# A new step order for a Mamba-2 decoder layer in fp32: output product ahead, decays one step later

## The chip, the cores and the metric

The kernel runs on one core of one Trainium2 chip. The metric is the time of one execution on the device, in microseconds. The engines are TensorE (PE; its weight loads are PEld), VectorE (DVE), ScalarE (ACT), GpSimd (POOL) and SyncE (SP), which here issues all transfers. Each engine runs its own instructions in the order written; they meet by semaphores.

## The reference

One decoder layer on x of 2 x 256 tokens by 512 features. It has a state-space attention (128 heads of 64, 8 groups of 16 heads), a quantised product with a context, and a block-diagonal GELU network behind a permutation. Nearly all the time is the first:

```
h = rmsnorm(x) * norm_w;  gate, hBC, dt = h @ in_proj_w.T
hBC = silu(causal_conv(hBC, 4 taps));  hid, B, C = hBC
dt = softplus(dt + dt_bias);  A = -exp(A_log)
M = (C B^T) * exp(segsum(A dt))          # per head, chunks of 128
y = M (hid dt) + C state exp(cumsum)  + D * hid
y = groupnorm(y * silu(gate)) * gnorm_w  # over the 1024 channels of a group
out = x + y @ out_proj_w.T
```

## The kernel before, in words

Channels lie on partitions, 512 tokens on the free axis. Each of the 8 groups has 8 tiles of 128 channels (CT = 8), so 64 steps of two heads each. The first and the last group are written out, groups 1 to 6 are one loop over n, with a body of the eight steps t. fp32 products are made of two fp32r parts: ScalarE rounds a weight tile (`cast`, L591; `cast_out`, L599), GpSimd subtracts to get the rest (`split`, L452; `split_out`, L462), and TensorE makes three products per pair (`split3`, L1147 to L1149). A projection is twelve matmuls of 128x512, an output product (`out_tile`) as many.

Step (n, t) holds stages of several tiles, each with a lag: `lagged(n, t, 2)` is the tile two steps back. For a tile the stages are: the projections of its hidden part h and its gate g; ScalarE's first tap (`tap0`, L611), VectorE's other three (L873), tanh (L618) and `conv_silu` (L882); TensorE's transpose (`turn`, L1217) and VectorE's `turned` (L900); the decay rows, loaded to `e` (L364), masked by GpSimd (`mask_rows`, L472), exponentiated by ScalarE (`exps`, L639), and multiplied by the scores, one third by GpSimd (`decays_off`, L483) and two thirds by VectorE (`decays_diagonal`, L926); the two heads' products (`outputs`, L1256 and L1259) into ps_y; `skip_and_gate` (L953 and L956); ScalarE's `z_high_and_square` (L646, L652), VectorE's `z_low` (L962), GpSimd's `add_square` (L490); and the output product into four banks that gather a group. At a group's end `token_sums` (L1268), `mean_square` (L967), `group_rms` (a pow, L494) and four `add_output` (L971) bring it to the residual. B and C of the next group are two more projections, in steps 3 and 5 (B_STEP, C_STEP). `masked_scores` (L911, L914) and `group_params` (L938, L939) belong to t = 0, the end of the group to t = 2.

The order of a step on each engine is written by hand in its `step` function. On TensorE: project h(t), turn(t-1), outputs(t-2), out_tile(t-3), project g(t), and B or C. On GpSimd: the splits of the next step's tiles, decays_off(t-1), split_out(t-2), mask_rows(t), add_square(t-2). On ScalarE: the tanh of g(t-1), casts of the next step's tiles, tap0(t), exps(t-1), tanh(t), z_high_and_square(t-2), cast_out(t-2). On VectorE: gated(t-1) (L892), taps(t), turned(t-1), skip_and_gate(t-2), conv_silu(t), z_low(t-2), decays_diagonal(t-1). Two PSUM banks (ps_in) take the projections in turn, so a projection waits until what used its bank two tiles ago is read (`bank_taken_from`). Rings: six weight tiles, four output weight tiles, four sets of rows.

In the first group GpSimd also rounds the quantised context (`context`, L502 to L506), one tile per step. Behind the last group it makes eight one-hot matrices (L567, L569) ahead of `group_rms`.

## Time and profile before

| | |
|---|---|
| median of 3 runs | 943.29 us (942.54 to 943.3) |
| the profiled execution | 941.07 us, span 939.3 us |
| TensorE busy | 821.1 us, 87% |
| VectorE busy | 696.5 us, 74% |
| GpSimd busy | 624.8 us, 67% |
| ScalarE busy | 542.9 us, 58% |
| mean granted clock of TensorE | 0.933 |

The span goes from the first to the last instruction. Busy shares are means over stretches with different limits, so they only say where to look. A row of a timeline gives the start and the length of an instruction (or of several of a kind that follow each other, with their count), and in brackets the idle time before it and what released it. A granted clock of 1.00 is 2.4 GHz, 0.50 is 1.2 GHz.

### The profile page before, as it was taken

How to read it: one execution, taken by the hardware profiler on the slowest of the kernel's cores; microseconds unless marked ns; L12 is line 12 of the kernel's file. 1: busy time of each engine (PE TensorE's matmuls, PEld its weight loads, DVE VectorE, ACT ScalarE, POOL GpSimd, SP SyncE). 2: the span in 40 equal slices, each digit the busy share in tenths (PEclk: the TensorE clock that was granted, in tenths of full speed). 3: DMA queues.
4: the chain of work that ended last, by engine and by line, in shares of the span. 5: the costliest groups of instructions: out<-in, count | busy, mean ns of one | idle time of the engine just before them, and what ended most of it. 6: DMA issues, size and time to landing. Idle time of an engine off the chain costs nothing.

```text
span 939.3 us, 14298 instructions
## 1 busy us (share of the span) xinstructions
PE 821.1 (87%) x4158; PEld 639.1 (68%) x4158; DVE 696.5 (74%) x912; ACT 542.9 (58%) x1124; POOL 624.8 (67%) x522
## 2 busy tenths in 40 slices
PE   4769898899989998999899998999899989994368
PEld 3547766677767776777677776777687767773155
DVE  6767578588958896797868895879589777672653
ACT  2357566465647664676656574666476665762253
POOL 3578999666856776576756785687667675767220
PEclk9889999899989998999989998999899999998579
DMA  5245344233434353433433343435243343300001
GB/s 189 90 152 201 115 145 146 90 135 123 150 100 147 108 169 107 145 131 126 145 109 133 112 148 134 134 106 172 79 145 134 127 142 124 116 31 22 1 0 45
DMA packets 44048, 111.11 MB, mean 118 GB/s; under 512 B 5748, under 2 KB 6644, under 8 KB 44020
## 3 DMA queue, kind: packets, MB, share of 16 engines
q1 hardware_dynamic: 44020, 110.76, 35.3%
q8 instruction: 14, 0.23, 0.1%
q14 instruction: 14, 0.11, 0.0%
HBM read 109.30 MB, written 1.44 MB: 118 GB/s over the span
## 4 chain that ended last, share of the span: by engine, by line
PE 45%; DVE 27%; issue 13%; ACT 7%; POOL 6%; DVEq 1%; DMA 0%; ACTq 0%; SPq 0%; POOLq 0%
PE ps_in L1147 9%; PE ps_in L1148 8%; PE ps_in L1149 8%; DVE hid L873 6%; PE ps_o L1147 4%; PE ps_o L1148 3%; PE ps_o L1149 3%; DVE z L956 3%; PE ps_y L1256 3%; DVE e L926 3%; DVE hdt L900 2%; DVE z L953 2%; ACT hid L611 2%; DVE bc L882 2%; PE ps_t L1217 1%
## 5 line engine op out<-in xcount | busy, mean ns | idle before, releaser
L1147 PE MATMUL ps_in<-h_hi,w_hi 128*128 128x512 f32 x560 | 232.2, 415 | 22.4 <-DVE gate L892 11.9
L1148 PE MATMUL ps_in<-h_lo,w_hi 128*128 128x512 f32 x560 | 228.4, 408 | 0.0
L1149 PE MATMUL ps_in<-h_hi,w_lo 128*128 128x512 f32 x560 | 227.8, 407 | 0.0
L462 POOL TENSOR_TENSOR wo_lo<-rawo,wo_hi 128x512 fp32r<-128x512 f32 x64 | 112.8, 1763 | 151.1 <-ACT wo_hi L599 97.5
L873 DVE SCALAR_TENSOR_TENSOR hid<-ps_in,curc,hid 128x510 f32<-128x510 f32 x186 | 138.9, 747 | 93.6 <-ACT hid L611 88.5
L452 POOL TENSOR_TENSOR w_lo<-raw,w_hi 128x512 fp32r<-128x512 f32 x144 | 188.9, 1332 | 15.7 <-ACT w_hi L591 15.6
L639 ACT ACTIVATE e<-e,nag 128x256 f32<-128x256 f32 (+1 forms) x512 | 183.6, 443 | 12.0 <-POOL e L472 12.0
L1147 PEld LDWEIGHTS ps_in<-h_hi,w_hi 128*128 128x128 f32 x560 | 111.2, 199 | 50.4 <-issue 24.2
L611 ACT ACTIVATE hid<-ps_in,curc 128x512 f32<-128x512 f32 x62 | 48.1, 776 | 150.4 <-PE ps_in L1149 139.4
L1149 PEld LDWEIGHTS ps_in<-h_hi,w_lo 128*128 128x128 f32 x560 | 111.4, 199 | 24.7
L1148 PEld LDWEIGHTS ps_in<-h_lo,w_hi 128*128 128x128 f32 x560 | 111.7, 199 | 22.9
L483 POOL TENSOR_TENSOR e<-e,gm 128x512 f32<-128x512 f32 x64 | 89.9, 1405 | 54.8 <-ACT e L639 54.7
L1147 PE MATMUL ps_o<-wo_hi,z_hi 128*128 128x512 f32 x256 | 107.7, 421 | 0.6 <-DVE gate L892 0.6
L646 ACT ACTIVATE z_hi<-z,curs 128x512 fp32r<-128x512 f32 x64 | 46.4, 725 | 103.4 <-DVE z L956 103.4
L1148 PE MATMUL ps_o<-wo_lo,z_hi 128*128 128x512 f32 x256 | 100.6, 393 | 0.0
L1149 PE MATMUL ps_o<-wo_hi,z_lo 128*128 128x512 f32 x256 | 100.5, 393 | 0.0
L926 DVE TENSOR_TENSOR e<-e,gm 128x1024 f32<-128x1024 f32 x64 | 93.2, 1457 | 4.4 <-ACT e L639 4.4
L472 POOL TENSOR_SCALAR_AFFINE_SELECT e<-e 128x512 f32<-128x512 f32 x128 | 91.7, 739 | 0.0
L1256 PE MATMUL ps_y<-e,hdt 128*64 128x256 f32 x512 | 81.2, 396 | 6.7 <-POOL e L483 6.4
L591 ACT ACTIVATE w_hi<-raw 128x512 fp32r<-128x512 f32 x144 | 84.3, 621 | 0.0
L490 POOL TENSOR_TENSOR sqsum<-sqsum,sq 128x512 f32<-128x512 f32 x56 | 71.8, 1283 | 6.6 <-ACT sq L652 6.6
L962 DVE SCALAR_TENSOR_TENSOR z_lo<-z,curs,z_hi 128x512 fp32r<-128x512 f32 x64 | 56.9, 889 | 12.9 <-ACT z_hi L646 12.9
(209 smaller groups left out, 1275.2 us busy)
## 6 DMA issues: line engine op xcount, KB each, us to landing
e<-acs_rows SPq DMA_DIRECT2D x64, 768.0 KB, 4.4
raw<-in_w_in SPq DMA_DIRECT2D x144, 256.0 KB, 4.7
rawo<-in_w_out SPq DMA_DIRECT2D x64, 256.0 KB, 2.6
craw<-in_ctx SPq DMA_DIRECT2D x8, 256.0 KB, 3.1
res<-in_x SPq DMA_DIRECT2D x4, 256.0 KB, 3.1
out_x<-res SPq DMA_DIRECT2D x4, 256.0 KB, 2.2
acs_rows<-z SPq DMA_DIRECT2D x3, 128.0 KB, 1.9
rawo<-in_w_dt SPq DMA_DIRECT2D x1, 256.0 KB, 4.3
```

What stands on the lines that cost most here:

```text
L452: pool.tensor_tensor(w_lo[:, slot, :], raw[:, slot, :], w_hi[:, slot, :].bitcast(F32), ALU.subtract).then_inc(s_lo, 1)
L462: pool.tensor_tensor(wo_lo[:, q % WO_RING, :], rawo[:, q % RAWO_RING, :], wo_hi[:, q % WO_RING, :].bitcast(F32), ALU.subtract).then_inc(s_ ...
L472: last = pool.affine_select(out=d, in_=d, compare_op=ALU.is_ge, fill=MASKED, base=0, pattern=[[0, 2], [0, BATCH], [1, P]], channel_multipl ...
L483: pool.tensor_tensor(o, o, gm[:, 1, :, :].rearrange("p b i -> p (b i)").unsqueeze(1) .broadcast_to([P, 2, BATCH * P]), ALU.mult).then_inc( ...
L591: act.activation(w_hi[:, slot, :], raw[:, slot, :], ACT.Copy).then_inc(s_hi, 1)
L639: last = act.activation(a, a, ACT.Exp, bias=nag[:, 2 * b + late, h:h + 1])
L873: last = dve.scalar_tensor_tensor(y[:, :, a:], src[:, :, 0:SEQ - a], par[:, at + 3 - a:at + 4 - a], y[:, :, a:], ALU.mult, ALU.add)
L926: dve.tensor_tensor(a, a, g, ALU.mult).then_inc(s_ma, 1)
L1147: pe.matmul(dst, lh, rh, start=first, stop=False)
L1148: pe.matmul(dst, lh, rl, start=False, stop=False)
L1149: return pe.matmul(dst, ll, rh, start=False, stop=last)
L1256: last = pe.matmul(ps_y[rows_, at:at + SEQ], w, e[:, q % E_RING, hh, 0:2, b, :], start=True, stop=False, skip_group_check=True)
```

## The change

The stages stay the same; their order and their lags change. The gate's projection moves a step back: step t projects h(t), then B or C (now at t = 4 and 6), then g(t-1). On TensorE the output product of t-3 goes ahead of turn(t-1) and outputs(t-2), the scores move to t = 1, and token_sums stands behind the outputs of t = 2. decays_off and decays_diagonal get a lag of 2, at the start of the step, gated as well; add_square a lag of 3. On ScalarE the second and third cast go behind z_high_and_square, cast_out ahead of tap0. On VectorE conv_silu(t) stands before skip_and_gate, masked_scores and group_params move to t = 1, mean_square to the end of t = 2, and the four add_output to t = 3, ahead of the taps. The context's three instructions per tile move from GpSimd in the first group to VectorE in the last, with the conversion of the permutation; the one-hot matrices move to VectorE, behind mean_square. The last square is no more added by GpSimd: the last token sums take both parts. The first group has four steps of lead instead of three, `LEAD` is one tile instead of two. SP loads input weights two steps ahead as before. `following(n, t)` is the list of step t+1's tiles; `extra_of(n, t)` names B or C.

```diff
-LEAD = 2
+LEAD = 1
...
-B_STEP, C_STEP = 3, 5
+B_STEP, C_STEP = 4, 6
...
 def step_tiles(n, t):
...
+    extra = extra_of(n, t)
+    back = (0, ("C0", 0)) if is_first(n) and t == 0 else (n, ("g", t - 1)) if t else (n - 1, ("g", CT - 1))
+    return [(n, ("h", t))] + ([(n, extra)] if extra else []) + [back]
...
             def step(n, t):
-                if t == 2 and not is_first(n):
+                tiles = following(n, t)
+                lead = is_first(n) and t < 4
+                if t == 3 and not is_first(n):
                     group_rms(n - 1)
-                ahead = (n, t + 1) if t + 1 < CT else (n + 1, 0)
-                tiles = [] if is_last(n) and t + 1 == CT else step_tiles(*ahead)
-                lead = is_first(n) and t < 3
-                if tiles:
-                    split_in(ahead[0], tiles[0])
-                m, q = lagged(n, t, 2)
-                if tiles:
-                    split_in(ahead[0], tiles[1])
...
+                if not lead:
+                    decays_off(*lagged(n, t, 2))
...
-                if not (is_first(n) and t < 2):
-                    decays_off(*lagged(n, t, 1))
-                    rows_arrived(n, t)
-                    split_out(m, q)
-                    mask_rows(n, t)
-                if len(tiles) > 2:
-                    split_in(ahead[0], tiles[2])
+                split_in(*tiles[0])
+                m, q = lagged(n, t, 3)
                 if q and not lead:
                     add_square(m, q)
...
+                if not (is_first(n) and t < 2):
+                    rows_arrived(n, t)
...
+                if len(tiles) > 1:
+                    split_in(*tiles[1])
...
+                if not (is_first(n) and t < 2):
+                    mask_rows(n, t)
+                if not lead:
+                    split_out(*lagged(n, t, 2))
+                if len(tiles) > 2:
+                    split_in(*tiles[2])
...
             def step(n, t):
-                ahead = (n, t + 1) if t + 1 < CT else (n + 1, 0)
-                tiles = [] if is_last(n) and t + 1 == CT else step_tiles(*ahead)
-                extra = {B_STEP + 1: ("B", B_STEP), C_STEP + 1: ("C", C_STEP)}.get(t)
-                extra = None if is_last(n) else extra
-                lead = is_first(n) and t < 3
-                m, q = lagged(n, t, 2)
-                if not (is_first(n) and t == 0):
-                    gate_tanh(*lagged(n, t, 1))
-                if tiles:
-                    cast_in(ahead[0], tiles[0])
-                if extra:
-                    tap0(n, extra)
-                if tiles:
-                    cast_in(ahead[0], tiles[1])
+                tiles = following(n, t)
+                extra, earlier = extra_of(n, t), extra_of(n, t - 1)
+                lead = is_first(n) and t < 4
+                if not (is_first(n) and t < 2):
+                    gate_tanh(*lagged(n, t, 2))
+                cast_in(*tiles[0])
+                if earlier:
+                    conv_tanh(n, earlier)
+                if not lead:
+                    cast_out(*lagged(n, t, 2))
                 tap0(n, ("h", t))
-                if extra:
-                    conv_tanh(n, extra)
...
                 if not lead:
                     exps(*lagged(n, t, 1))
                 conv_tanh(n, ("h", t))
...
+                if extra:
+                    tap0(n, extra)
                 if not lead:
-                    z_high_and_square(m, q)
+                    z_high_and_square(*lagged(n, t, 2))
+                for tile in tiles[1:]:
+                    cast_in(*tile)
...
             def step(n, t):
-                extra = {B_STEP + 1: ("B", B_STEP), C_STEP + 1: ("C", C_STEP)}.get(t)
-                extra = None if is_last(n) else extra
-                lead = is_first(n) and t < 3
-                m, q = lagged(n, t, 2)
-                if t == 0:
+                extra, earlier = extra_of(n, t), extra_of(n, t - 1)
+                lead = is_first(n) and t < 4
+                if t == 0 and not is_first(n):
                     conv_params(n)
                 if t == 2:
-                    if not is_first(n):
-                        mean_square(n - 1)
                     ssd_params(n)
-                if not (is_first(n) and t == 0):
-                    gated(*lagged(n, t, 1))
-                if extra:
-                    taps(n, extra)
+                if not (is_first(n) and t < 2):
+                    gated(*lagged(n, t, 2))
+                if t == 1 and not is_first(n):
+                    group_params(n)
+                if not lead:
+                    decays_diagonal(*lagged(n, t, 2))
+                if earlier:
+                    conv_silu(n, earlier)
+                if t == 3 and not is_first(n):
+                    dve.wait_ge(s_r, n)
+                    dve.wait_ge(s_ou, CT * n)
+                    for k in range(TT):
+                        add_output(k)
...
                 taps(n, ("h", t))
-                if extra:
-                    conv_silu(n, extra)
...
                 if not lead:
                     turned(*lagged(n, t, 1))
-                    skip_and_gate(m, q)
-                conv_silu(n, ("h", t))
...
+                conv_silu(n, ("h", t))
+                if not lead:
+                    skip_and_gate(*lagged(n, t, 2))
...
                 if not lead:
-                    z_low(m, q)
-                    decays_diagonal(*lagged(n, t, 1))
-                if t == 0 and not is_first(n):
-                    group_params(n)
+                    z_low(*lagged(n, t, 2))
+                if extra:
+                    taps(n, extra)
+                if t == 1 and not is_first(n) or t == 2 and is_first(n):
                     masked_scores(n)
                 if t == 2 and not is_first(n):
-                    dve.wait_ge(s_r, n)
-                    dve.wait_ge(s_ou, CT * n)
-                    for k in range(TT):
-                        if is_first(n - 1):
-                            dve.wait_ge(s_res, TT)
-                        add_output(k)
...
+                    mean_square(n - 1)
+                if is_last(n):
+                    context(t)
...
             last_m = GROUPS - 1
+            gated(last_m, CT - 2)
+            decays_diagonal(last_m, CT - 2)
+            turned(last_m, CT - 1)
             skip_and_gate(last_m, CT - 2)
-            gated(last_m, CT - 1)
-            turned(last_m, CT - 1)
             decays_diagonal(last_m, CT - 1)
             z_low(last_m, CT - 2)
+            gated(last_m, CT - 1)
             skip_and_gate(last_m, CT - 1)
             z_low(last_m, CT - 1)
             mean_square(last_m)
+            for k in range(DK):
+                one_hot(k)
...
             def token_sums(m):
 
+                pe.wait_ge(s_tf, CT * (m + 1) + 2)
                 pe.wait_ge(s_sqs, (CT - 1) * (m + 1))
-                pe.wait_ge(s_tf, min(CT * (m + 1) + 1, STEPS) if isinstance(m, int) else CT * (m + 1) + 1)
...
             def step(n, t):
                 tiles = step_tiles(n, t)
-                lead = is_first(n) and t < 3
+                lead = is_first(n) and t < 4
+                project(*tiles[0])
...
+                if not lead:
+                    out_tile(*lagged(n, t, 3))
+                    turn(*lagged(n, t, 1))
+                    outputs(*lagged(n, t, 2))
+                for tile in tiles[1:-1]:
+                    project(*tile)
+                if t == 1 and not is_first(n):
+                    scores(n)
                 if t == 2 and not is_first(n):
                     token_sums(n - 1)
-                project(n, tiles[0])
-                if is_first(n) and t == 1:
-                    dt_turn()
+                project(*tiles[-1])
...
-                if not lead:
-                    turn(*lagged(n, t, 1))
-                    outputs(*lagged(n, t, 2))
-                    out_tile(*lagged(n, t, 3))
-                if t == 0 and not lead:
-                    scores(n)
-                for tile in tiles[1:]:
-                    project(n, tile)
...
             last_m = GROUPS - 1
+            turn(last_m, CT - 1)
             outputs(last_m, CT - 2)
-            turn(last_m, CT - 1)
+            project(last_m, ("g", CT - 1))
             out_tile(last_m, CT - 3)
+            outputs(last_m, CT - 1)
+            out_tile(last_m, CT - 2)
...
-            outputs(last_m, CT - 1)
-            out_tile(last_m, CT - 2)
-            token_sums(last_m)
+            last_token_sums()
             out_tile(last_m, CT - 1)
```

## Rows read from the trace of the kernel before

**Rows 1.** TensorE's timeline, outputs of steps. Columns: start us, us, engine, line, operation.

```profile
88.93 0.65 PE L1256 MATMUL ps_y<-e,hdt 128*64 128x256 f32 x4
...
142.22 0.65 PE L1256 MATMUL ps_y<-e,hdt 128*64 128x256 f32 x4 [0.66 <-POOL e L483]
...
478.96 0.65 PE L1256 MATMUL ps_y<-e,hdt 128*64 128x256 f32 x4
...
489.25 0.65 PE L1256 MATMUL ps_y<-e,hdt 128*64 128x256 f32 x4
...
502.25 0.65 PE L1256 MATMUL ps_y<-e,hdt 128*64 128x256 f32 x4
...
751.50 0.65 PE L1256 MATMUL ps_y<-e,hdt 128*64 128x256 f32 x4
...
839.24 0.65 PE L1256 MATMUL ps_y<-e,hdt 128*64 128x256 f32 x4 [0.37 <-issue]
...
840.34 0.42 PE L1259 MATMUL ps_y<-e,hdt 128*64 128x128 f32 x4
```

**Rows 2.** Busy times by stretch: us, PE, PEld, DVE, ACT, POOL, then clock and DMA.

```profile
44.90:139.00 94.10, 79.34 (x382) 61.44 (x381) 63.66 (x89) 55.88 (x119) 83.57 (x66) 0.91 0.46 159
...
444.60:546.50 101.90, 95.43 (x497) 75.39 (x496) 81.89 (x102) 64.81 (x138) 70.80 (x59) 0.97 0.39 129
```

**Rows 3.** TensorE's timeline at two waits, and two stretches by time (granted clock: PEclk).

```profile
471.62 1.86 PE L1268 MATMUL ps_t<-ones,sqsum 128*128 128x1 f32 x8 [3.85 <-POOL sqsum L490]
...
524.40 0.49 PE L1147 MATMUL ps_in<-h_hi,w_hi 128*128 128x512 f32 x1 [1.98 <-DVE gate L892]
...
477.30:479.30 2.00, 2.00 (x12) 1.44 (x12) 0.00 (x0) 0.59 (x1) 0.00 (x0) 0.77 0.00 0
...
422.40:427.00 4.60, 4.51 (x13) 3.47 (x14) 2.11 (x3) 0.00 (x0) 4.18 (x4) 0.63 0.11 44
```

**Rows 4.** GpSimd's timeline in one step.

```profile
458.43 1.22 POOL L472 TENSOR_SCALAR_AFFINE_SELECT e<-e 128x512 f32<-128x512 f32 x2
...
460.85 2.53 POOL L452 TENSOR_TENSOR w_lo<-raw,w_hi 128x512 fp32r<-128x512 f32 x2
...
463.35 1.29 POOL L483 TENSOR_TENSOR e<-e,gm 128x512 f32<-128x512 f32 x1
```

**Rows 5.** GpSimd's and VectorE's timelines around 139 us.

```profile
136.75 3.00 POOL L452 TENSOR_TENSOR w_lo<-raw,w_hi 128x512 fp32r<-128x512 f32 x2
...
138.52 2.32 DVE L926 TENSOR_TENSOR e<-e,gm 128x1024 f32<-128x1024 f32 x1
...
139.72 2.25 POOL L483 TENSOR_TENSOR e<-e,gm 128x512 f32<-128x512 f32 x1
```

**Rows 6.** ScalarE's timeline in one step.

```profile
478.71 0.78 ACT L611 ACTIVATE hid<-ps_in,curc 128x512 f32<-128x512 f32 x1 [9.27 <-PE ps_in L1149]
...
483.85 0.73 ACT L646 ACTIVATE z_hi<-z,curs 128x512 fp32r<-128x512 f32 x1 [1.07 <-DVE z L956]
...
485.00 0.61 ACT L599 ACTIVATE wo_hi<-rawo 128x512 fp32r<-128x512 f32 x1
```

**Rows 7.** VectorE's lines, ns min/median/max; the taps from its timeline.

```profile
L956 DVE TENSOR_TENSOR z<-z,gate x64: 691/882/1671, 71.9 to 855.2; 128x512 f32<-128x512 f32 x64
...
L926 DVE TENSOR_TENSOR e<-e,gm x64: 1210/1218/2318, 66.2 to 847.3; 128x1024 f32<-128x1024 f32 x64
...
L953 DVE SCALAR_TENSOR_TENSOR z<-hid,curs,ps_y x64: 730/739/748, 71.2 to 854.5; 128x512 f32<-128x512 f32 x64
...
479.52 2.31 DVE L873 SCALAR_TENSOR_TENSOR hid<-ps_in,curc,hid 128x510 f32<-128x510 f32 x3 [4.85 <-ACT hid L611]
...
L938 DVE COPY dtg<-dtT x8: 600/1288/1294, 56.6 to 760.2; 128x64 f32 x6, 128x64 f32<-128x64 f32 x2
...
L1074 DVE TENSOR_SCALAR e<-e x4: 420/424/427, 879.3 to 883.3; 128x512 f32<-128x512 f32 x4
```

**Rows 8.** VectorE's timeline behind the last group.

```profile
872.02 1.41 DVE L971 SCALAR_TENSOR_TENSOR res<-ps_o,rgrp,res 128x512 f32<-128x512 f32 x2 [12.09 <-POOL rgrp L494]
```

More of the change, by code:

```diff
@@ L52, in is_last, with extra_of, before @@
     return isinstance(n, int) and n == GROUPS - 1
-def step_tiles(n, t):
-    extra = {B_STEP: ["B"], C_STEP: ["C"]}.get(t, [])
-    return [("h", t), ("g", t)] + ([] if is_last(n) else [(x, t) for x in extra])
-def body_tiles(n):
-    return [tile for t in range(CT) for tile in step_tiles(n, t)]
-def tile_index(n, tile):
-    return LEAD + NIN * n + body_tiles(n).index(tile)
+def extra_of(n, t):
+    if is_last(n):
+        return None
+    return {B_STEP: ("B", t), C_STEP: ("C", t)}.get(t)
+def before(n):
+    return n - 1
@@ new lines, in body_tiles, with place, ring_index, conv_order @@
+def body_tiles(n):
+    return [tile for t in range(CT) for _, tile in step_tiles(n, t)] + ([("g", CT)] if is_last(n) else [])
+def place(n, tile):
+    if tile == ("g", CT - 1):
+        return (n, NIN - 2) if is_last(n) else (n + 1, 1)
+    return n, body_tiles(n).index(tile)
+def ring_index(n, tile):
+    return 0 if tile[0] == "B0" else LEAD + place(n, tile)[1]
+def tile_index(n, tile):
+    return 0 if tile[0] == "B0" else NIN * place(n, tile)[0] + ring_index(n, tile)
+def conv_order(n, tile):
+    if tile[0] == "B0":
+        return 0
+    order = [x for x in body_tiles(n) if x[0] != "g"].index(tile)
+    return order + (1 if is_first(n) else LEAD_CONV)
@@ L544, in _ @@
-            for j in range(2):
-                split(j, j)
+                if not (is_first(n) and t < 2):
+                    rows_arrived(n, t)
+                    if is_first(n) and t == 2:
+                        rows_arrived(0, 0)
+                        rows_arrived(0, 1)
+                if len(tiles) > 1:
+                    split_in(*tiles[1])
+                if is_first(n) and t == 0:
+                    for k in range(TT):
+                        start_residual(k)
+                if is_first(n) and t == 2:
+                    mask_rows(0, 0)
+                    mask_rows(0, 1)
@@ L546, in _ @@
+                if not (is_first(n) and t < 2):
[4 more added lines that the diff above has]
+                    split_in(*tiles[2])
+                if is_first(n) and t == 3:
+                    split_out(0, 0)
+                    decays_off(0, 1)
+                    split_out(0, 1)
+            split(0, 0)
             for tile in step_tiles(0, 0):
-                split_in(0, tile)
+                split_in(*tile)
@@ L556, in _ @@
             last_m = GROUPS - 1
-            add_square(last_m, CT - 2)
+            decays_off(last_m, CT - 2)
+            add_square(last_m, CT - 3)
             split_out(last_m, CT - 2)
@@ L560, in _ @@
             split_out(last_m, CT - 1)
[L561 to L570 removed]
+            add_square(last_m, CT - 2)
             group_rms(last_m)
@@ L908, in masked_scores @@
                 wait(dve, s_mb, CT * n)
+                wait(dve, s_ma, CT * n)
                 dve.wait_ge(s_sc, 2 * n + 1)
@@ L1230, in scores @@
                 last.then_inc(s_sc, 1)
[L1231 removed]
+                wait(pe, s_z1, CT * n)
                 for b in range(BATCH):
@@ L1269, in token_sums, with last_token_sums @@
                                      start=True, stop=True)
+                last.then_inc(s_ss, 1)
+            def last_token_sums():
+                pe.wait_ge(s_tf, STEPS)
+                pe.wait_ge(s_sqs, (CT - 1) * GROUPS - 1)
+                pe.wait_ge(s_sq, STEPS)
+                for t in range(TT):
+                    for part in (sqsum, sq):
+                        last = pe.matmul(ps_t[:, t:t + 1], part[:, t * P:(t + 1) * P], ones[:, :],
+                                         start=(part is sqsum), stop=(part is sq))
                 last.then_inc(s_ss, 1)
```

306 lines of the change are left out of this document (167 added, 139 removed).

## The prediction

> **What bounds the kernel now.** I read the stretches first. A loop group (eight steps) takes 101.6 us: the outputs of group 1 begin at 142.22 and those of group 7 at 751.50, so 609.3 us for six groups [rows 1]. TensorE is busy 95.4 of 101.9 us in such a group, VectorE 81.9, GpSimd 70.8 [rows 2]; so TensorE is the nearest bound, with gaps. Its timeline shows an undisturbed step: 478.96 to 489.25, 10.3 us; one with a third projection lasts 13.0 (489.25 to 502.25), so a projection is 2.7 us [rows 1]. The rest of the 10.3 is a second projection, the output product (2.8, as many matmuls), the turn (0.5) and the outputs (as 839.24 to 840.76, 1.5). Eight steps, two more projections, and some 2.4 for scores and token sums make 90.2; the other 11.4 us are waits and what follows them. The longest is the token sums' for the last sum of squares: 3.9 us, after which the clock stands at half (1.2 GHz) until about 478, a loss of some 3.4 more; a projection waits 2.0 us for a gate [rows 3]. So up to 11 us a group are to be had, if no other engine's order takes them.
>
> **The loop after the change.** The token sums now wait for a square added one slot earlier and stand behind the outputs; their 3.9 us and the slow stretch go. The output product of t-3 stands right behind the projection and covers the wait for the decays. But the decays are now made in the step that uses them: before, GpSimd's decays_off and VectorE's decays_diagonal had a lag of 1 against the outputs' 2; now all have 2. And GpSimd splits the gate's weights (the second tile of the next step) in front of the mask, split_out and the next decays_off, while ScalarE casts that tile only behind z_high_and_square. That closes a ring, once per step: cast, GpSimd's split, mask, split_out, decays_off, TensorE's outputs, VectorE's skip and gate, ScalarE's z_hi and square, the next cast.
>
> Its length: split 1.25 (two in 2.53), mask 1.2, split_out 1.25 (the same subtraction), decays_off 1.3, together 5.0 [rows 4]. To TensorE it is 0.25: decays_off of 139.72 ends at 141.97 and the outputs start at 142.22 [rows 1, 5]. Outputs 1.5 [rows 1]. z_hi, square and a copy take 1.75 (483.85 to 485.61) [rows 6]. Skip 0.75 and gate product 0.7 [rows 7]. With 0.15 for the other hand-overs the ring is 10.1, just under the 10.3 of TensorE. That would hide it. What breaks it is a collision: decays_diagonal, gate product, silu and z_low never run beside a GpSimd instruction. decays_diagonal started at 138.52 during two splits, took 2.32 instead of 1.21 and ended at 140.84; decays_off, started at 139.72, took 2.25 instead of 1.3 [rows 5, 7]. The Trainium skill (SBUF — State Buffer, "SBUF: two separate sides") says so: the port pair that VectorE and GpSimd share is an exclusive lock, and whichever starts first holds it for its whole instruction. By that, the trace agrees, no overlap of these two is to be had; a sum that let them overlap would stay at 10.3 a step, which is the first rival below.
>
> In the new order decays_diagonal of t-1 becomes ready some 1.2 us behind the cast (one instruction of ScalarE and one of VectorE), when GpSimd has begun its 5.0 us in a row, so its 1.1 us enter the ring: 11.2. The gate product meets add_square, between 0 and 0.55 (its instructions last 0.69 to 1.67 [rows 7]); I take 0.3, nearer to the median of 0.88. A normal step is thus 11.5, and TensorE waits 1.2 in each.
>
> The other steps, from cast to cast. **t=1**: two copies of group parameters (0.6 alone, 1.29 in collision [rows 7]) fall in GpSimd's row: +1.1, 12.6. **t=2**: the second half of the scores must await skip_and_gate of the last tile in the same step, which makes projections and masked_scores late: 12.0. **t=3**: the four add_outputs now stand before the taps, and the output product, moved ahead, waits for them. They wait for GpSimd's pow, which follows split, diagonal, mask and split_out: 0.1+1.25+1.1+1.2+1.25+1.0 = 5.9. The first addition is done at 6.7, TensorE has been idle since 2.5: 4.2 us, more than the 3.9 that brought the half clock before [rows 3]. Product, turn and outputs then take 4.8 at full clock and 7.6 at half, skip, gate and the three ScalarE instructions 3.3: 15.0 to 17.7, I take 16.5. **t=4 and 6** (B and C): one more split in the ring, so the outputs end at 9.1; ScalarE's tap 0 of the extra tile comes before z_hi and needs its projection: 9.1+2.7+0.2+0.7+1.75+0.1 = 14.6 [rows 1, 6]. **t=5 and 7**: h(t) takes the bank of B or C, whose taps (2.3 [rows 7]) end about 1.9 behind the cast; then 2.7+2.8+0.5+1.5, then 3.3: 12.7, with silu's collision 12.8. With 11.5 for t=0 the group is 11.5+12.6+12.0+16.5+14.6+12.8+14.6+12.8 = 107.4, against 101.6. Six of them: +35. Ends: 104.5 without the gate's collision and at full clock, 110 with both in full.
>
> DMAs: on SP the loads stay two steps ahead, load_rows no longer waits behind anything new, and the rings have their old depth; I cost them at nothing, hidden by that lead. If it went, a cast would start late, and the ring with it.
>
> **First group.** GpSimd was its bound (83.6 of 94.1 us busy [rows 2]): four steps, 88.93 to 142.22, took 53.3 [rows 1]. It loses the context work. But by the sums above the same four take 14.6+12.8+14.6+12.8 = 54.8. Ahead of them GpSimd's waits shrink, and one more step is filled by hand; I take 2.5 off, so -1 in all, with -10 and +6 as ends.
>
> **Last group.** Before, from outputs at 751.50 to those at 839.24, 87.7 us [rows 1]. After: no B and C, 11.5+12.6+12.0+16.5+4x11.5 = 98.6, and each step has three context instructions on VectorE, of 0.42 each [rows 7], of which two fall in GpSimd's row: 8x0.85 = 6.8. 105.4, so +18. The parameters converted once before it are a few short instructions, within the error.
>
> **Tail.** Before, 31.3 us from the end of the outputs at 840.8 to the first addition at 872.02, whose wait for the pow was 12.1 [rows 8], since eight one-hot instructions on GpSimd stood before it. After: projection 2.7, product 2.8, outputs 1.5, product 2.8, eight column sums at a product's 0.23 each, token sums 0.8 (an estimate), then mean square and eight one-hots of 0.42 on VectorE, while GpSimd does the pow: 16.2. -15. What follows is unchanged.
>
> **Sum.** -1 +35 +18 -15 = +37 on the profiled execution's 941.1 us (939.3 of span and 1.8 around it): 978. That execution is 2.2 below the median of the runs, so 980. Its own range, by the ends of group and lead, is 950 to 1005.
>
> **Rivals.**
> *TensorE sets the pace.* The ring stays under 10.3 because decays_diagonal finds a gap of GpSimd; it decides at 1.0 us off my 11.5. Then only step 3's wait is left: 90.2+4.2+3.4 = 97.8 a group, -3.8 in each of seven, -7 in the first group (its four steps at 46.6), -15 in the tail: -49, so 894. For it: the ring without collisions is 10.1, and before, 0.69 to 0.88 was usual for the gate product. Against: GpSimd's 7.5 us a step (six instructions) and VectorE's 3.0 (four) that exclude each other already add to 10.5. Partly so, it gives up to 938. 0.31.
> *The clock falls in every step.* The 1.2 us waits come each step and those of t=5 and 7 are 1.9, near the 2.0 after which the window from 422.40 has a mean clock of 0.63 [rows 3]. At half for four us a step costs TensorE 2.3, of which 1.2 is slack: +1.1 a step, 44 more: 1024. Against: one wait of 2.0 (524.40) was passed at full clock. The Trainium skill (TensorE: Matmul & The Clock Gate, "HAM oscillation") describes loops that fall back in every iteration. 0.09.
> *It cancels.* The stalls taken and those put in are equal and the change does nothing in sum: a group of about 102 and contexts hidden, 941 to 945. 0.05.
>
> **Numbers.** The forecast has 0.55. With the clock's 0.09, slower is 0.64; faster 0.31; within 0.2% (what a measurement of this kernel can tell from no change) 0.05. For 8 in 10 the range must take in most of the first rival: 900 to 1008.
>
> **What would show it.** Right: outputs 11.2 to 11.8 us apart in normal steps, waiting for decays_off; GpSimd idle before the gate's split, released by ScalarE's cast; TensorE idle about 4 us before the output product of t=3, released by add_output, then half clock; no wait at the token sums; add_output after the loop within 17 us of the last loop's outputs. Wrong: steps of 10.3 with TensorE busy throughout, or waits of TensorE that name another engine than GpSimd in normal steps.

## The result, and the profile after

| | before | after |
|---|---|---|
| median of the runs | 942.91 us (941.76 to 943.3, 4 runs) | 1067.2 us (1061.11 to 1070.62, 4 runs) |
| the profiled execution | 941.07 us, span 939.3 us | 1070.62 us, span 1068.9 us |
| mean granted clock of TensorE | 0.933 | 0.912 |

The ratio is 1.1313, 95% interval 1.126 to 1.1367. The change makes the kernel 124 us slower. The prediction had the sign (slower, 0.64) but 980 us and a range to 1008: the result lies far outside.

The page's first part, kernel after (busy time, share of the span, instructions):

```profile
span 1068.9 us, 14301 instructions
## 1 busy us (share of the span) xinstructions
PE 863.9 (81%) x4164; PEld 658.1 (62%) x4166; DVE 690.1 (65%) x943; ACT 544.5 (51%) x1124; POOL 586.2 (55%) x489
```

No engine is full now. TensorE has 43 us more of busy time for the same work. Some 31 of them are matmuls at half clock: 293 of the 128x512 ones start 0.43 us behind the one before them instead of 0.23, against 138 in the kernel before. The rest of what was added to the span is waiting. In the rows below, w_lo is what GpSimd's split of the input weights makes, wo_lo its split of the output weights, z VectorE's gate product, z_hi ScalarE's rounding of it, hdt VectorE's `turned`, e the decays. The waits of the kernel after, longest first in total (us in total, times, longest):

```profile
POOL w_lo L505 <- ACT w_hi L628: 330.5, 54, 10.0
ACT z_hi L690 <- DVE z L1024: 181.5, 50, 7.6
DVE hdt L966 <- PE ps_t L1298: 126.6, 49, 5.4
...
PE ps_o L1225 <- POOL wo_lo L515: 87.3, 38, 3.1
```

Read together they name a circle: GpSimd waits for ScalarE's cast, ScalarE for VectorE's gate product, VectorE for TensorE's turn, TensorE for GpSimd's split of the output weights (`split_out`, L515). The last link is the new one. Here is the circle in the step t=1 of a loop group, engine by engine. TensorE (start, length, in brackets the idle time before and its releaser):

```profile
524.26 0.47 PE L1225 MATMUL ps_o<-wo_hi,z_hi 128*128 128x512 f32 x1 [2.75 <-POOL wo_lo L515]
...
527.11 0.60 PE L1298 MATMUL ps_t<-ident,hid 128*128 128x128 f32 x4
527.64 0.65 PE L1336 MATMUL ps_y<-e,hdt 128*64 128x256 f32 x4
...
537.46 0.47 PE L1225 MATMUL ps_o<-wo_hi,z_hi 128*128 128x512 f32 x1 [1.26 <-POOL wo_lo L515]
```

VectorE, then ScalarE, then GpSimd in the same step:

```profile
529.21 0.75 DVE L1021 SCALAR_TENSOR_TENSOR z<-hid,curs,ps_y 128x512 f32<-128x512 f32 x1
529.99 0.69 DVE L1024 TENSOR_TENSOR z<-z,gate 128x512 f32<-128x512 f32 x1
...
534.83 1.37 DVE L993 TENSOR_TENSOR e<-e,gm 128x1024 f32<-128x1024 f32 x1
```

```profile
530.72 0.72 ACT L690 ACTIVATE z_hi<-z,curs 128x512 fp32r<-128x512 f32 x1 [4.77 <-DVE z L1024]
531.34 0.62 ACT L696 ACTIVATE sq<-z 128x512 f32<-128x512 f32 x1
531.87 0.62 ACT L628 ACTIVATE w_hi<-raw 128x512 fp32r<-128x512 f32 x1
```

```profile
532.64 1.29 POOL L505 TENSOR_TENSOR w_lo<-raw,w_hi 128x512 fp32r<-128x512 f32 x1 [4.78 <-ACT w_hi L628]
533.88 1.24 POOL L525 TENSOR_SCALAR_AFFINE_SELECT e<-e 128x512 f32<-128x512 f32 x2
535.08 2.23 POOL L515 TENSOR_TENSOR wo_lo<-rawo,wo_hi 128x512 fp32r<-128x512 f32 x1
537.28 1.29 POOL L536 TENSOR_TENSOR e<-e,gm 128x512 f32<-128x512 f32 x1
```

From one product to the next, by starts: product, turn and outputs until the skip, 524.26 to 529.21, 4.95 us; skip, gate product, z_hi, square and cast until the split, to 532.64, 3.43; split, mask and split_out until the product, to 537.46, 4.82. Together 13.2. decays_off (537.28) is not in it: it runs beside the product. split_out, due at 535.08, overlaps VectorE's decays_diagonal (L993, 534.83 to 536.20) and took 2.23 us instead of the 1.27 of a step in which it does not.

**By stretches.** Outputs begin at t=4 of the first group, at the start of the loop, of the last group, and behind it (the row of t=0 of the last group is 869.81):

```profile
93.70 0.65 PE L1336 MATMUL ps_y<-e,hdt 128*64 128x256 f32 x4
...
155.27 0.65 PE L1336 MATMUL ps_y<-e,hdt 128*64 128x256 f32 x4
...
869.81 0.65 PE L1336 MATMUL ps_y<-e,hdt 128*64 128x256 f32 x4
...
979.96 0.88 PE L1336 MATMUL ps_y<-e,hdt 128*64 128x256 f32 x4 [4.06 <-issue]
```

| stretch | before [rows 1] | after | difference | predicted |
|---|---|---|---|---|
| up to the loop's first outputs | 142.22 | 155.27 | +13.0 | -1 |
| six groups of the loop | 609.3 | 714.5 | +105.3 | +35 |
| last group | 87.7 | 110.2 | +22.4 | +18 |
| behind it, to the end | 100.1 | 88.9 | -11.1 | -15 |

The differences add up to +129.6, the difference of the spans. (The profiled execution of after is the slowest of its four, 3.4 us over the median.)

### The profile page after: what moved, and what is told of

Its sections match the earlier page's. It is cut to its first block and busy times, and to the rows that moved or that the text cites. A ratio compares the mean times of both kernels' runs of the same rounds, so it can differ in the third digit from the quotient of the medians.

```text
span 1068.9 us, 14301 instructions
## 1 busy us (share of the span) xinstructions
PE 863.9 (81%) x4164; PEld 658.1 (62%) x4166; DVE 690.1 (65%) x943; ACT 544.5 (51%) x1124; POOL 586.2 (55%) x489
## 5 line engine op out<-in xcount | busy, mean ns | idle before, releaser
L1226 PE MATMUL ps_in<-h_lo,w_hi 128*128 128x512 f32 x560 | 223.9, 400 | 0.0
L1227 PE MATMUL ps_in<-h_hi,w_lo 128*128 128x512 f32 x560 | 223.5, 399 | 0.0
L1225 PE MATMUL ps_o<-wo_hi,z_hi 128*128 128x512 f32 x256 | 122.6, 479 | 112.3 <-POOL wo_lo L515 87.3
L683 ACT ACTIVATE e<-e,nag 128x256 f32<-128x256 f32 (+1 forms) x512 | 183.6, 443 | 14.1 <-POOL e L525 11.5
L1225 PEld LDWEIGHTS ps_o<-wo_hi,z_hi 128*128 128x128 f32 x256 | 58.0, 227 | 145.2 <-issue 109.4
L966 DVE TENSOR_TENSOR hdt<-ps_t,dtg 128x512 f32<-128x512 f32 x64 | 44.2, 691 | 127.1 <-PE ps_t L1298 126.6
L1227 PE MATMUL ps_o<-wo_hi,z_lo 128*128 128x512 f32 x256 | 118.5, 463 | 0.0
L1226 PE MATMUL ps_o<-wo_lo,z_hi 128*128 128x512 f32 x256 | 118.2, 462 | 0.0
L515 POOL TENSOR_TENSOR wo_lo<-rawo,wo_hi 128x512 fp32r<-128x512 f32 x64 | 109.5, 1711 | 6.3 <-ACT wo_hi L636 6.3
L525 POOL TENSOR_SCALAR_AFFINE_SELECT e<-e 128x512 f32<-128x512 f32 x128 | 107.5, 864 | 0.0
L1030 DVE SCALAR_TENSOR_TENSOR z_lo<-z,curs,z_hi 128x512 fp32r<-128x512 f32 x64 | 48.7, 760 | 80.2 <-ACT z_hi L690 80.2
L536 POOL TENSOR_TENSOR e<-e,gm 128x512 f32<-128x512 f32 x64 | 94.2, 1472 | 0.0
L993 DVE TENSOR_TENSOR e<-e,gm 128x1024 f32<-128x1024 f32 x64 | 93.6, 1462 | 0.8
L628 ACT ACTIVATE w_hi<-raw 128x512 fp32r<-128x512 f32 x144 | 87.5, 618 | 11.5 <-DMA raw<-in_w_in 11.5
```

The source lines that it names most:

```text
L515: pool.tensor_tensor(wo_lo[:, q % WO_RING, :], rawo[:, q % RAWO_RING, :], wo_hi[:, q % WO_RING, :].bitcast(F32), ALU.subtract).then_inc(s_ ...
L525: last = pool.affine_select(out=d, in_=d, compare_op=ALU.is_ge, fill=MASKED, base=0, pattern=[[0, 2], [0, BATCH], [1, P]], channel_multipl ...
L536: pool.tensor_tensor(o, o, gm[:, 1, :, :].rearrange("p b i -> p (b i)").unsqueeze(1) .broadcast_to([P, 2, BATCH * P]), ALU.mult).then_inc( ...
L628: act.activation(w_hi[:, slot, :], raw[:, slot, :], ACT.Copy).then_inc(s_hi, 1)
L683: last = act.activation(a, a, ACT.Exp, bias=nag[:, 2 * b + late, h:h + 1])
L993: dve.tensor_tensor(a, a, g, ALU.mult).then_inc(s_ma, 1)
```

## The experiments

Twelve kernels were run. The first three each undo one part of the change on the kernel after. Ratios are to the kernel before, which took 942.4 to 943.1 us in the same rounds.

**a1_cast_early**: ScalarE's later casts ahead of z_high_and_square.

```diff
                 conv_tanh(n, ("h", t))
+                for tile in tiles[1:]:
+                    cast_in(*tile)
...
-                for tile in tiles[1:]:
-                    cast_in(*tile)
```

> The changed kernel with one thing moved: ScalarE casts the second and third tile of the next step right behind the tanh of h(t), no more behind z_high_and_square. Theory R (a ring of waits, one turn per step: cast, GpSimd's split, mask, split_out, TensorE's output product, turn, outputs, VectorE's skip and gate, ScalarE's z_hi and square, next cast; 0.1+1.25+1.1+1.2+1.25+0.25+2.8+0.5+1.5+0.75+0.7+0.1+1.75 = 13.2 us): the ring is cut, normal steps fall to 10.3 to 10.8 us, the time to 915 to 950. Theory L (VectorE and GpSimd shut each other out, whatever the order): steps stay above 12.5, time above 1030. Theory C (the waits only cost so much because the clock falls): no more than 30 us less.

Measured: 951.61 us (947.38 to 954.55), ratio to before 1.0087 [1.0054, 1.0121]: 116 us faster than the change as it is, and 1.6 us above the range expected by the theory of the ring. Normal steps stand 10.3 us apart again, without a wait. TensorE's outputs in a1_cast_early:

```profile
509.98 0.65 PE L1336 MATMUL ps_y<-e,hdt 128*64 128x256 f32 x4
...
520.27 0.65 PE L1336 MATMUL ps_y<-e,hdt 128*64 128x256 f32 x4
...
529.70 0.49 PE L1225 MATMUL ps_in<-h_hi,w_hi 128*128 128x512 f32 x1 [2.22 <-DVE bc L939]
...
537.38 0.65 PE L1336 MATMUL ps_y<-e,hdt 128*64 128x256 f32 x4
```

The same rows show what is left: a step with B or C lasts 17.1 us here (15.8 to 17.5 in the loop), not 13.0, and the projection of h behind it waits 2.2 us for VectorE's taps of B or C. The waits of the output product for add_output, 24.9 us in the kernel after, are 5.4 here: most of the stall at t=3 hung on the late cast too.

**a2_splitout_early**: GpSimd's split_out(t-2) right behind decays_off, so that it no longer stands behind the late cast's split.

```diff
                     decays_off(*lagged(n, t, 2))
+                    split_out(*lagged(n, t, 2))
...
-                if not lead:
-                    split_out(*lagged(n, t, 2))
```

> The changed kernel with one thing moved: GpSimd's split_out of t-2 stands right behind decays_off, ahead of the splits. Theory R: the output product no longer waits, and what is left is the ring over decays_off without split_out, 0.1+1.25+1.1+1.2+1.3+0.25+1.5+0.75+0.7+0.1+1.75 = 10.0 us, under TensorE's 10.3: time 920 to 955. Theory L: as before the move, above 1030. If instead the cast's place alone matters, about 1060.

Measured: 959.62 us (958.64 to 961.32), ratio 1.0185 [1.0165, 1.0205]. The circle is cut at another link, at nearly the same gain: 108 us. The time is 4.6 us above the range expected. TensorE no longer waits for wo_lo at all.

**a3_product_behind**: the output product of t-3 behind turn and outputs.

```diff
-                    out_tile(*lagged(n, t, 3))
                     turn(*lagged(n, t, 1))
                     outputs(*lagged(n, t, 2))
+                    out_tile(*lagged(n, t, 3))
```

> The changed kernel with one thing undone: TensorE's output product of t-3 stands behind the outputs again. Theory R: the product and the turn ahead of it leave the ring's way, what is left is the ring that the prediction reckoned, 11.2 to 11.7 us a normal step, group about 107: time 965 to 990. Theory L: above 1030. A theory that the wait for the additions in t = 3 is the greater part: it goes here too, so under 950.

Measured: 1081.13 us (1073.07 to 1087.29), ratio 1.1461 [1.1391, 1.1531]. A miss: undoing the very part that made TensorE wait for split_out brought nothing. The waits of a3_product_behind show the circle closed through decays_off instead, and a new wait for the gate's projection:

```profile
POOL w_lo L505 <- ACT w_hi L628: 340.5, 55, 12.6
...
PE ps_y L1336 <- POOL e L536: 85.9, 31, 4.8
...
ACT gth L670 <- PE ps_in L1227: 57.9, 47, 3.7
```

VectorE's timeline around the outputs of 533.67 (their end 535.2) shows why the circle did not get shorter by the product's 2.8:

```profile
533.49 2.30 DVE L939 SCALAR_TENSOR_TENSOR hid<-ps_in,curc,hid 128x510 f32<-128x510 f32 x3
535.70 0.68 DVE L966 TENSOR_TENSOR hdt<-ps_t,dtg 128x512 f32<-128x512 f32 x1
536.56 0.69 DVE L948 SCALAR_TENSOR_TENSOR hid<-th,hid 128x512 f32<-128x512 f32 x1 [0.18 <-ACT th L655]
537.17 0.74 DVE L1021 SCALAR_TENSOR_TENSOR z<-hid,curs,ps_y 128x512 f32<-128x512 f32 x1
...
542.98 0.69 DVE L958 SCALAR_TENSOR_TENSOR gate<-gth,ps_in 128x512 f32<-128x512 f32 x1 [1.07 <-ACT gth L670]
```

The skip begins 2.0 us behind the outputs' end, since it stands behind taps, turned and silu of h(t); the taps stand behind gated and decays_diagonal, which wait for the projection of the gate, which on TensorE now stands behind the product. By this reading a longer circle over two steps has formed. The next two kernels each cut a piece out of it.

**a6_behind_and_cast_early**: the edits of a3 and of a1 together.

> The kernel after with two edits at once: the output product behind the turn and the outputs (as in a3_product_behind), and ScalarE's casts of the later tiles behind conv_tanh(h t) (as in a1_cast_early). Theory R2 (a3 gained nothing because its path is then a second ring over two steps, outputs, product, projection of g, gate tanh, gated, decays_diagonal, taps, tanh, silu, skip, gate product, z_hi, square, cast, GpSimd's four, outputs, some 26.4 us for two steps; the cast behind the tanh cuts silu, skip, gate product, z_hi and square out of it, about 3.4 to 4 us): two steps take at most 23, and the time comes to 925 to 965. Rival (the product's place behind the outputs costs for itself, because nothing then covers the decays on TensorE): within 20 us of a3's 1081. Time: 945.

Measured: 1023.36 us (1020.73 to 1024.91), ratio 1.0848 [1.0827, 1.0869]. Between the two expectations, and a miss for both: the cast still gives 58 us, but it is 72 us behind a1, from which it differs by the product's place alone. Outputs still wait for decays_off, up to 4.0 us:

```profile
PE ps_y L1336 <- POOL e L536: 40.9, 14, 4.0
```

The longest of these waits, 3.98 us before the outputs of 537.41, can be followed back. GpSimd's row ahead of it begins at 529.09 with a split that waits for ScalarE's cast, and the cast stands behind the tanh of h(t), which waits for VectorE's taps:

```profile
527.86 0.63 ACT L655 ACTIVATE th<-hid 128x512 f32<-128x512 f32 x1 [2.08 <-DVE hid L939]
```

The taps (525.54 to 527.83) stand behind four add_output, decays_diagonal and gated, and gated waits for the tanh of the gate's projection, which on TensorE stands behind the product. So the early cast is still in a path that holds the product: ahead of the outputs the product would be beside this path, behind them it is in it. How much of the 72 us is this was not separated.

**a7_behind_and_skip_early**: a3's edit, and VectorE's skip ahead of the silu.

```diff
+                if not lead:
+                    skip_and_gate(*lagged(n, t, 2))
                 conv_silu(n, ("h", t))
-                if not lead:
-                    skip_and_gate(*lagged(n, t, 2))
```

> The kernel after with the output product behind the outputs (as in a3_product_behind) and VectorE's skip_and_gate ahead of conv_silu(h t), the order of before. Theory R2: of the second ring only silu and the wait for its tanh go (0.7 + 0.3 us per two steps), since the skip stays behind the taps and turned: 1035 to 1065. Rival (the skip's place behind the silu was what undid a3): below 990. Time: 1050.

Measured: 1057.2 us (1049.35 to 1060.75), ratio 1.1223 [1.1198, 1.1249]. It lies in the range that the circle over two steps gave: the skip's place is worth 24 us, and is not what undid a3.

**c3_before_cast_late** and **c4_before_product_ahead** put the same parts, one each, into the kernel before.

```diff
-                if tiles:
+                if tiles and lead:
                     cast_in(ahead[0], tiles[1])
...
                     z_high_and_square(m, q)
+                if tiles and not lead:
+                    cast_in(ahead[0], tiles[1])
```

> The kernel before with one part of the change alone: ScalarE casts the gate's tile (and B, C) behind z_high_and_square, not ahead of tap0. Theory R (the late cast costs because the decays and the output weights of the same step stand behind its split): here decays_off has a lag of 1, so the circle is outputs 1.5, skip 0.75, gate product 0.7, z_hi, square and cast 1.75, split 1.25, decays_off 1.3 to 2.25, hand-overs 0.4, in all 7.7 to 8.6 us, under TensorE's 10.3: 940 to 957. Rival (the late cast is harmful by itself, since it makes every projection of a gate late): above 975. Time: 948.

Measured: 955.49 us (955.01 to 955.9), ratio 1.0132 [1.0112, 1.0152], at the upper edge of what the theory allowed.

```diff
+                    out_tile(*lagged(n, t, 3))
                     turn(*lagged(n, t, 1))
                     outputs(*lagged(n, t, 2))
-                    out_tile(*lagged(n, t, 3))
```

> The kernel before with another part alone: TensorE's output product of t-3 ahead of turn and outputs. Before, the decays are ready a step early, so there is nothing for it to cover; the output weights split in the step before are ready too. The outputs come 2.8 us later in the step, which nothing waits for in a ring (7.7 us and less). At t=3 the product must wait for add_output earlier than before, 0 to 2 us in each of 7 groups. Theory: 940 to 960. Rival (a product ahead costs wherever it stands, as it makes skip, gate and z late): above 970. Time: 948.

Measured: 958.3 us (956.03 to 958.54), ratio 1.0156 [1.0132, 1.0179]. So neither part is dear by itself: +13 and +16 us against the 942.43 us of the kernel before in the same rounds. TensorE's waits in c3, then in c4:

```profile
PE ps_t L1270 <- POOL sqsum L490: 43.5, 8, 6.2
...
PE ps_y L1258 <- POOL e L483: 14.6, 24, 5.7
```

```profile
PE ps_t L1268 <- POOL sqsum L490: 35.4, 8, 5.2
...
PE ps_o L1147 <- POOL wo_lo L462: 14.0, 17, 2.6
```

The token sums wait longer for the last square (28.0 us in the kernel before). And the two links are both there in small: in c4 the product ahead already waits for wo_lo, 17 times, which never happened with the product behind. The two parts by themselves make 29 us, so most of the 124 comes from parts together. Late cast and product ahead together in the old order were not run, so how much of it the later decays add is not shown.

**b1_onehot_vector** and **b3_before_sums_and_onehots** put the change's good parts into the kernel before: the one-hots on VectorE alone, then with the group's end one step later as well.

```diff
             mean_square(last_m)
...
+            for k in range(DK):
+                dve.tensor_scalar(take[:, k, :], perm_row[:, :], dcol[:, k:k + 1], None, ALU.is_equal)\
...
+                dve.tensor_scalar(put[:, k, :], iota_row[:, :], perm_col[:, k:k + 1], None, ALU.is_equal)\
...
```

> The kernel before with only the eight one-hot matrices moved from GpSimd to VectorE, behind mean_square. Step of the sum on the tail: the wait of 12.1 us for the pow becomes 8 x 0.42 = 3.4 and 0.3: 8 to 9 us less, 932 to 935. If the one-hots take 1.56 each on VectorE as on GpSimd, no more than 1 us less.

Measured: 933.25 us (931.2 to 934.99), ratio 0.9901 [0.9875, 0.9926]. A one-hot is 0.48 us on VectorE there, 1.56 on GpSimd before, and the kernel gains 9.7 us.

```diff
-                if t == 2 and not is_first(n):
-                    token_sums(n - 1)
                 project(n, tiles[0])
...
                     outputs(*lagged(n, t, 2))
+                    if t == 2 and not is_first(n):
+                        token_sums(n - 1)
                     out_tile(*lagged(n, t, 3))
...
-                if t == 2 and not is_first(n):
+                if t == 3 and not is_first(n):
                     group_rms(n - 1)
...
+                if t == 3 and not is_first(n):
+                    dve.wait_ge(s_r, n)
+                    dve.wait_ge(s_ou, CT * n)
+                    for k in range(TT):
...
+                        add_output(k)
```

> Of the change only what needs no new order of the decays, on the kernel before: the one-hots on VectorE (b1_onehot_vector, -9.7 us), and the end of a group one step later: token_sums behind the outputs of t=2, mean_square at the end of t=2, group_rms and the four add_output at t=3. The wait for the last square (3.9 us in each of 7 groups) and the half clock behind it (3.4) go; the next output product (tile 0 of the new group) may wait for add_output instead. Theory: 880 to 905 if the product's wait stays under 1 us. Rival (the wait moves to add_output, as in the kernel after): 920 to 940. Time: 893.

Measured: 904.62 us (902.15 to 906.06), ratio 0.9585 [0.9565, 0.9604]: 38 us faster than before. The stall of the token sums and the slow stretch behind it are what the change was right to attack; in the old order of the decays they can be had without the circle. The stall is not all gone in b3: the token sums wait 2.0 us for VectorE's `turned` there, 14.3 us in seven times, where they waited 28.0 us for the last square.

**a8_cast_and_taps_early**, **a10_contexts_behind_taps** and **a11_all_and_split_out_early** repair the new order step by step. First a1, and the taps of B and C ahead of z_low:

```diff
+                if extra:
+                    taps(n, extra)
                 if not lead:
                     z_low(*lagged(n, t, 2))
-                if extra:
-                    taps(n, extra)
```

> The kernel a1_cast_early (951.6) with VectorE's taps of B and C ahead of z_low. Theory B (in a1 the steps t=4 and t=6 last 17 instead of 13 us because the projection of h(t+1) waits 2.2 us for the bank of B or C, whose taps stand behind z_low, which waits 1.8 us for ScalarE's z_hi, and TensorE then runs 4 us at half clock): the wait shrinks to about 0.4 and stays at full clock, 3.4 us less for each of 14 such steps, 905 to 925. Rival (VectorE or GpSimd is full in those steps and takes it back): 940 or more. Time: 915.

Measured: 917.09 us (916.57 to 918.8), ratio 0.9723 [0.9707, 0.9739]. Steps with B or C last 13.9 instead of 15.8 to 17.5. Then the contexts from the end of the step to behind the taps:

```diff
                 taps(n, ("h", t))
+                if is_last(n):
+                    context(t)
...
-                if is_last(n):
-                    context(t)
```

> The kernel a8_cast_and_taps_early (917.1) with VectorE's three context instructions of a step of the last group right behind the taps, where GpSimd is idle (789.2 to 793.9 us in a8), and no longer at the end of the step. In a8 they take 1.50, 1.40 and 1.40 us each there, and end when a GpSimd instruction ends; VectorE is full, the step lasts 13.5. Theory L (each of these instructions needs what a running GpSimd instruction holds, so it starts only between two of them): behind the taps they take 0.42 to 0.5 each, the step comes to 11 to 11.7, 12 to 18 us less in all, 899 to 905. Rival (the instruction costs 1.4 us for itself, in this form): they stay at 1.1 or more each and the time within 5 us of 917. Time: 902.

Measured: 906.19 us (903.36 to 907.93), ratio 0.9606 [0.9577, 0.9634], 1.2 us above the range. Up to the outputs at 733 us the two traces differ by 0.4 us, at the last outputs by 12.3, so the gain lies in the last group. VectorE's context instructions in a8, at the end of the step:

```profile
797.26 1.50 DVE L916 TENSOR_SCALAR craw<-craw,qd,qs 128x512 f32<-128x512 f32 x1
798.79 1.40 DVE L918 TENSOR_SCALAR craw<-craw 128x512 f32<-128x512 f32 x1
800.23 1.40 DVE L920 TENSOR_SCALAR q<-craw 128x512 bf16<-128x512 f32 x1
```

and GpSimd's in the same stretch of a8:

```profile
796.76 1.71 POOL L515 TENSOR_TENSOR wo_lo<-rawo,wo_hi 128x512 fp32r<-128x512 f32 x1
798.44 1.47 POOL L536 TENSOR_TENSOR e<-e,gm 128x512 f32<-128x512 f32 x1
799.87 1.47 POOL L505 TENSOR_TENSOR w_lo<-raw,w_hi 128x512 fp32r<-128x512 f32 x1
```

and VectorE's in a10, where GpSimd is idle (its next instruction starts at 750.97):

```profile
749.30 0.54 DVE L916 TENSOR_SCALAR craw<-craw,qd,qs 128x512 f32<-128x512 f32 x1
749.87 0.43 DVE L918 TENSOR_SCALAR craw<-craw 128x512 f32<-128x512 f32 x1
750.33 0.43 DVE L920 TENSOR_SCALAR q<-craw 128x512 bf16<-128x512 f32 x1
```

The instructions are the same. Next to a GpSimd row the second and third last three times as long, and each of the three ends 0.3 us behind the end of one of GpSimd's (798.76, 800.19 and 801.63 against 798.47, 799.91 and 801.34): as if each had waited for a gap between two of them. Last, split_out behind decays_off on top of it:

> The kernel a10_contexts_behind_taps with GpSimd's split_out(t-2) right behind decays_off as well (as in a2_splitout_early). With the casts early the output weights are no longer late: TensorE waits for wo_lo 3.0 us in sum over the whole of a8, 1.0 in each step of the last group. Theory R: within 5 us of a10, at most the 1.0 of each step of the last group less. Rival (the split of the output weights still sets the pace of some steps of every group): 10 us or more below a10. Time: 900.

Measured: 902.21 us (901.03 to 903.07), ratio 0.9572 [0.9553, 0.9591]: 4 us below a10, within the 5 us expected of a link that is no longer in the circle. With b3 it is the fastest version of the study; b3's 904.62 and its 902.21 are 0.3% apart.

## Why the prediction was wrong

**What held.** A ring of waits exists, through all four engines and closed by the late cast, and it sets every normal step. All of its links but two were named; the two are the step that failed, below. GpSimd stands idle 4.8 us before the gate's split, released by ScalarE's cast (532.64 above). The token sums wait for nothing. At t=3 the product waits for add_output 3.43 us (4.2 forecast). It starts at full clock, and from 553.6 the clock is at half for 3 us. The step from z_hi to z_hi lasts 16.5, the number forecast. TensorE at that product, and the clock of the stretch behind it:

```profile
552.32 0.50 PE L1225 MATMUL ps_o<-wo_hi,z_hi 128*128 128x512 f32 x1 [3.43 <-DVE res L1039]
```

```profile
552.30:556.60 4.30, 4.28 (x13) 3.23 (x14) 4.09 (x6) 0.27 (x2) 1.69 (x2) 0.65 0.09 36
```

The first add_output behind the last group starts at 999.91, 17.4 us behind the end (982.54) of the outputs that begin at 979.96; 16.2 were forecast, 17 was named as the limit, and 31.3 were needed before; these outputs themselves ran at half clock, 1.1 longer, and what follows the addition took 1.7 longer, so the gain is 11.1, not 15.

**The step that failed** is one sentence: "The output product of t-3 stands right behind the projection and covers the wait for the decays." It does cover it, and so takes decays_off's place in the ring. The product needs the rest of the output weights, and split_out(t-2) of the step before is the third piece of work behind the late cast (split, mask, split_out): TensorE's wait is `ps_o <- wo_lo`, 38 times and 87.3 us in sum, and not the forecast one for decays_off, `ps_y <- e`, which came once, for 1.6 us. The sum had split, mask, split_out, decays_off and then the outputs: 11.2. The trace has split, mask, split_out, then product (2.85) and turn (0.53), then the outputs; decays_off (1.3) runs beside. 11.2 - 1.3 + 2.85 + 0.53 is 13.3, measured 13.2. (The 0.3 that the forecast of 11.5 had for a collision of the gate product did not come: it took 0.69 in this step.) I had followed what the outputs wait for and not what the instruction moved ahead of them waits for.

**The second term that was missed** is what the clock does to a ring that has TensorE's work in it. At half clock the product lasts 1.4 us longer: from the product of 509.54, at half, to that of 524.26 it is 14.7, and from there, at full, 13.2. In the group of the table below the products of t=4, t=6 and the next t=0 (567.08, 597.13 and 628.73) are at half, 4.4 us instead of 2.85; so some 4.7 of the 12 us that a group lacks are the clock's. The rival "the clock falls in every step" priced that with a slack of 1.2 us a step on TensorE; there was none, because the product itself was in the ring. (It also had 2.3 us as the price of four us at half, where four us cost 2.0.) So a part of that rival came true on top of the forecast, not in its place.

By steps, from ScalarE's z_hi to the next in a loop group (517.49, 530.72, 543.89, 560.37, 577.25, 590.44, 607.25, 621.96, 636.82). A column holds the time up to the z_hi of its step; the first start is that of t=0, and the column t=0 is the last difference:

| | t=0 | t=1 | t=2 | t=3 | t=4 | t=5 | t=6 | t=7 | sum |
|---|---|---|---|---|---|---|---|---|---|
| forecast | 11.5 | 12.6 | 12.0 | 16.5 | 14.6 | 12.8 | 14.6 | 12.8 | 107.4 |
| measured | 14.9 | 13.2 | 13.2 | 16.5 | 16.9 | 13.2 | 16.8 | 14.7 | 119.3 |

The six groups lack 12 us each by this, some 70 of the 93 us by which the spans differ more than was forecast. The **first group** (-1 forecast, +13) is the same error: its four steps to the loop took 61.6, not 54.8, and the lead 4.8 longer instead of 2.5 shorter. The **last group** (+18, measured +22) is right only in sum: its steps, too, went by the longer ring, and the contexts, put at 0.42 each, took 0.73, 1.25 and 0.70 on average (8 of each), 21.4 us in all; how much of that lengthened this group was not separated in the kernel after. The collision of decays_diagonal (1.1 in the ring) held: split_out took 2.23, 1.0 more than alone. The Trainium skill (SBUF — State Buffer, "SBUF: two separate sides") has it as an exclusive lock on the port pair that VectorE and GpSimd share: whichever starts first has it for its whole instruction, and the other waits. The contexts in a8 and a10, 1.40 against 0.43, agree.

**What is shown and what is argued.** That the late cast and split_out behind it make the circle is shown by a1 and a2, that the late cast and the product ahead are cheap, each alone in the old order, by c3 and c4 (+13 and +16 us). What the new place of the decays adds was not tried by itself. That the product has to stay ahead once the casts are early is shown by a6 against a1 (72 us). The circle over two steps in a3 is read from its trace and not shown by a run: a7 agrees with it in size, but a6 came 58 us above the upper end of its expectation, so its length, and whether it is all that holds a3 and a6 back, stay open. What fixes when the clock falls was not tried.

## What to carry to other kernels

When an instruction is moved ahead, follow what it waits for itself, back to the step before, and not only what it will cover: here a product and a turn (3.4 us) took the place of a 1.3 us link in a circle, by way of a split that the product needs. A circle through all engines is paid once per step, here with no engine over 81% busy, and is best broken where a link hangs on another only by the order of an engine (a cast behind z, a split behind a split): either of two such moves of a single stage gave back 108 and 116 us. And test parts in pairs before calling one harmless: in the new order the product ahead gained 14 us with the cast late and 72 with it early, while in the old order it cost 16; the late cast cost 13 us in the old order and 116 in the new.

## What the runs showed of the hardware

- The three `tensor_scalar` of a context (128x512) on VectorE took 0.54, 0.43 and 0.43 us with GpSimd idle (a10) and 1.50, 1.40 and 1.40 beside a row of GpSimd's instructions, which became 1.47 long themselves instead of 1.29 (a8). Such work is not hidden beside a busy GpSimd: it lengthens both. The taps, which read PSUM, took 2.28 to 2.31 for three in either kernel.
- Two waits of the same length were followed by different clocks. These are the kernel after's rows: the product behind the first wait (the one behind the second, at 524.26, is shown above), and the busy times by stretch (PE, PEld, DVE, ACT, POOL, then clock) right behind each:

```profile
509.54 0.76 PE L1225 MATMUL ps_o<-wo_hi,z_hi 128*128 128x512 f32 x1 [2.76 <-POOL wo_lo L515]
```

```profile
509.60:512.20 2.60, 2.60 (x6) 2.06 (x7) 0.50 (x1) 1.98 (x6) 2.60 (x3) 0.50 0.40 101
524.40:527.00 2.60, 2.60 (x12) 2.12 (x13) 0.77 (x2) 1.40 (x4) 2.60 (x3) 1.00 0.39 101
```

  After 2.76 us of idling the product ran at 0.50, after 2.75 us at 1.00. In both cases the engine had been busy at 1.00 ahead of the wait (504.00 to 506.70, 518.00 to 521.50). Behind the wait of 3.43 us at t=3 the product started at 1.00 and fell to 0.50 1.3 us later. The length of a wait alone does not tell the clock behind it.
